# A gated cross-attention and a quantised feed-forward stage in one program block: general path first, two tiles in the last batch's attention

## The chip, the cores and the metric

The kernel runs on one core of a Trainium2 chip. The metric is device microseconds from the start to the end of one execution; lower is better. The engines are named PE (matmul), PEld (its weight load), DVE, ACT, POOL (GpSimd) and SP, which here only issues DMAs.

## What is computed

```python
def bitlinear(x, w, b):
    xq = act_quant(rmsnorm(x))          # 8 bit levels per row
    wq = weight_quant(w)                # -1, 0, 1 times a mean
    return einsum('bsd,fd->bsf', xq, wq) + b
# x: (32, 224, 512), ctx: (32, 750, 384), 16 heads of 32
q = layernorm(x) @ Wq.T;  k, v = ctx @ Wkv.T
attn = where(pad_mask[:, None, :, None], q @ k.T * scale, -1e9)
x = x + tanh(g_xattn) * softmax(attn) @ v
x = x + tanh(g_ffn) * bitlinear(gelu(bitlinear(layernorm(x), w1, b1)), w2, b2)
```

The mask is per query row, and a masked row gets the mean of v. In the inputs that are timed only rows from 168 on can be unmasked, which is the last quarter of a batch.

## The kernel before

**Attention stage.** A batch of 224 rows is four blocks of 56 (`NBLK`, `R`). In each batch only the last block (`RB`), together with one row of zeros that gives the mean of v, is attended; two batches share one tile of x (`xa`, 114 rows). `period(b, j, t, late)` on each engine does batch b's attention and, woven into it, batch b+1's projection to k and v. The projections and scores split each fp32 operand into a high and a low part (`y_h`, `y_l`, `wkv_h`, `wkv_l`, `k_h`, `k_l`), three matmuls each. `batches` calls `period` for all 32 batches; the last two are written out. The last has no projection to do. Heads come in four groups, and for each group the order is: scores on PE; the maxima on DVE (`negated_max`); exp on ACT (`softmax`); transposes of prob on PE (`turn_prob`); their copies to `prob_t` by ACT (`first_half`) and DVE (`second_half`); `weighted` sums on PE; `heads_out` on DVE. `sums` and `divided` end a batch. PE's scores of group g+1 wait for both copies of group g.

POOL and DVE also normalise the previous batch's rows for the feed-forward stage (`summed`, `centred`, `rounded`, `x1_moments`, `x1_peak`) and SP stores them in DRAM as x1 rows and quantised xq rows. In the second half POOL also rounds the weights (`weights`) into `w_q`, one piece a batch.

**General path.** A batch with unmasked rows in other blocks goes through `slow`, which is held in a loop over 32 batches behind two tests (class `Slow`). `most` is the largest of the flags `kind`; each engine loads it and jumps over the loop if it is at most 1, as it is here. `most` comes from the mask by a DVE reduction (`live_b`), a DMA that brings that onto one partition (`live`), and three small DVE operations. In the kernel before, these three stand behind `wkv_l` on DVE, and `Slow` stands at the end of the first block.

**Feed-forward stage.** It is a second `nc.Block`, behind a barrier, over 56 tiles of 128 rows. In step s, PE widens tile s (16 matmuls, L1556), transposes tile s-2's integers (L1566), transposes the next input (L1575), and narrows tile s-3 (16 matmuls, L1583). DVE copies the widened halves to `hid` (L1498), ACT applies GELU (L1455), takes the integers (L1462) and the squares (L1468). Widening needs `xq_t` of the tile, and `hid` needs `b1_row`, the bias in all partitions (1024 KB) times a factor. A tile's xq is 128 KB and its x1 256.5 KB.

Every engine runs its instructions in the order of the code, and all waits are on semaphores. SP is one queue too: its DMAs go out in the order in which it meets them. Its first are y (1125 KB), two halves of wkv (768 KB each), wq (1024 KB), two gates (0.5 KB each), b2 (224 KB), and then `live` (0.5 KB).

## Time and profile before

| | us |
|---|---|
| median of three runs | 1872.94 (1870.43 to 1877.92) |
| the profiled execution | 1872.22 |
| its span | 1870.4 |
| PE busy | 1807.6 |
| DVE / ACT / POOL busy | 1155.2 / 990.6 / 791.2 |

All times in the rows further down are counted from the start of the span. Three stretches matter: the first 20 us, in which inputs land and PE starts; 1348 to 1427 us, from the start of the last batch's attention to the feed-forward tile 4; and the long steady loops on both sides of it.

### The profile page before, as it was taken

Reading aid. Unit: us, or ns where it says so; the run is one execution under the profiler, and the core shown is the slowest. Engines: PE = TensorE matmul, PEld = TensorE weight load, DVE = VectorE, ACT = ScalarE, POOL = GpSimd, SP = SyncE. Lnnn points to the kernel's source line nnn. Section 1 sums busy time; section 2 is a strip of 40 time slices with the busy share of each in tenths; the row PEclk is TensorE's granted clock in tenths of the full one; section 3 lists DMA queues with packets and bytes.
Section 4 is the critical chain, followed back from the end, with each engine's and each line's share of the span. In section 5 each row is a group of like instructions: output and inputs, shape, how many; then the busy total and the mean of one; then the engine's idle time right before and its main releaser. Section 6 shows DMA issues by size and latency. Waiting matters only on the chain. (4 is left out here: it accounts for less than half of the span.)

```text
span 1870.4 us, 46291 instructions
## 1 busy us (share of the span) xinstructions
PE 1807.6 (97%) x16938; PEld 1396.5 (75%) x16995; DVE 1155.2 (62%) x2015; ACT 990.6 (53%) x1639; POOL 791.2 (42%) x1091
## 2 busy tenths in 40 slices
PE   6999999999999999999999999999958999999998
PEld 6888888888888888888888888888834555555554
DVE  3555655555555655555555555555448888888885
ACT  3444444444444443444444444444327888888886
POOL 1134454443344453665556565655444222222222
PEclk9999999999999999999999999999979999999999
DMA  4132222322332222322332222322242222222221
GB/s 157 35 96 85 73 78 73 92 73 80 117 89 78 73 78 75 94 73 78 110 93 83 73 78 73 92 73 78 66 132 66 80 85 81 76 82 84 81 75 45
DMA packets 83697, 154.24 MB, mean 82 GB/s; under 512 B 9726, under 2 KB 24062, under 8 KB 83510
## 3 DMA queue, kind: packets, MB, share of 16 engines
q1 hardware_dynamic: 83310, 153.24, 27.2%
q8 instruction: 33, 0.54, 0.1%
q10 hardware_dynamic: 328, 0.25, 0.1%
q14 instruction: 26, 0.21, 0.0%
HBM read 112.99 MB, written 40.81 MB: 82 GB/s over the span
## 5 line engine op out<-in xcount | busy, mean ns | idle before, releaser
L593 ACT ACTIVATE prob<-psum,nmax 114x750 f32<-114x750 f32 x256 | 225.5, 885 | 268.0 <-DVE nmax L766 268.0
L771 DVE TENSOR_TENSOR k_l<-psum,k_h 128x376 fp32r<-128x376 f32 (+1 forms) x256 | 139.8, 546 | 286.7 <-ACT k_h L584 286.7
L766 DVE TENSOR_REDUCE nmax<-psum 114x1 f32<-114x750 f32 x256 | 228.5, 934 | 80.2 <-PE psum L1025 79.4
L1036 PE MATMUL psum<-y_h,wkv_h 128*128 128x376 f32 (+1 forms) x768 | 276.7, 360 | 1.1 <-DVE q_l L759 1.1
L584 ACT ACTIVATE k_h<-psum 128x376 fp32r<-128x376 f32 (+1 forms) x256 | 123.9, 484 | 280.7 <-PE psum L1036 280.0
L1036 PE MATMUL psum<-y_l,wkv_h 128*128 128x376 f32 (+1 forms) x768 | 255.6, 333 | 0.0
L1036 PE MATMUL psum<-y_h,wkv_l 128*128 128x376 f32 (+1 forms) x768 | 255.4, 333 | 0.0
L1046 PE MATMUL psum<-wkv_h,y_h 128*125 128x512 f32 x576 | 237.8, 413 | 0.7 <-DVE wkv_l L823 0.7
L264 POOL TENSOR_TENSOR f_x<-f_c,f_x 112x512 f32<-112x512 f32 x64 | 76.3, 1193 | 361.0 <-DMA f_c<-vmean_rows 337.6
L1046 PE MATMUL psum<-wkv_l,y_h 128*125 128x512 f32 x576 | 228.8, 397 | 0.0
L1046 PE MATMUL psum<-wkv_h,y_l 128*125 128x512 f32 x576 | 228.0, 396 | 0.0
L1556 PE MATMUL psum<-w_q,xq_t 128*128 128x512 bf16 x894 | 207.3, 386 | 9.5 <-DVE xq_t L1527 9.3
L1056 PEld LDWEIGHTS psum<-ident,prob 114*125 114x125 f32 x1536 | 187.2, 190 | 12.0 <-ACT prob L593 3.3
L1583 PE MATMUL psum<-w_q,hq_t 128*128 128x512 bf16 x842 | 191.1, 379 | 5.1 <-ACT yo L1477 2.2
L1056 PE MATMUL psum<-ident,prob 114*125 114x114 f32 x1536 | 190.2, 274 | 4.8 <-ACT prob L593 4.8
L780 DVE COPY prob_t<-psum 125x342 f32<-125x342 f32 x256 | 128.4, 512 | 104.3 <-PE psum L1056 93.5
L1556 PEld LDWEIGHTS psum<-w_q,xq_t 128*128 128x128 bf16 x896 | 85.0, 99 | 126.4 <-issue 22.3
L1455 ACT ACTIVATE hid<-hid,gelu_in 128x1024 f32<-128x1024 f32 x112 | 128.0, 1144 | 83.8 <-DVE hid L1498 83.5
L459 POOL TENSOR_TENSOR y_l<-y,y_h 128x750 fp32r<-128x750 f32 x93 | 151.0, 1650 | 26.4 <-ACT y_h L579 26.4
L1423 POOL TENSOR_SCALAR cols<-cols 128x1 f32<-128x1 f32 x56 | 10.7, 191 | 346.8 <-ACT junk L1468 346.8
L1583 PEld LDWEIGHTS psum<-w_q,hq_t 128*128 128x128 bf16 x896 | 85.2, 98 | 95.4 <-ACT yo L1477 2.8
L1036 PEld LDWEIGHTS psum<-y_h,wkv_h 128*128 128x128 f32 x768 | 144.6, 188 | 14.6 <-DVE q_l L759 1.5
(120 smaller groups left out, 3372.7 us busy)
## 6 DMA issues: line engine op xcount, KB each, us to landing
y<-in_ctx_t SPq DMA_DIRECT2D x32, 1125.0 KB, 5.7
w_part<-in_w_t SPq DMA_DIRECT2D x32, 512.0 KB, 7.1
x_rows<-f_x SPq DMA_DIRECT2D x64, 224.4 KB, 2.7
x<-x_rows SPq DMA_DIRECT2D x56, 256.5 KB, 2.7
f_x<-in_x SPq DMA_DIRECT2D x64, 224.0 KB, 5.4
out_rows<-yo SPq DMA_DIRECT2D x56, 256.0 KB, 2.1
xq_rows<-f_q SPq DMA_DIRECT2D x64, 112.0 KB, 2.6
xq<-xq_rows SPq DMA_DIRECT2D x56, 128.0 KB, 2.2
```

The costliest lines, as they stand in the source:

```text
L459: pool.tensor_tensor(y_l[:, slot, c, :], y[:, c, :], y_h[:, slot, c, :].bitcast(F32), ALU.subtract).then_inc(a_yl, 1)
L584: act.activation(k_h[:, g, s0:s1], ps_proj[k_bank[par][g, hf]][:, 0:s1 - s0], ACT.Copy).then_inc(a_kh, 1)
L593: act.activation(prob[:, e, :], ps_score[e][0:RP], ACT.Exp, bias=nmax[:, i:i + 1], accum_out=den[:, i:i + 1]).then_inc(p.exp, 1)
L766: dve.tensor_reduce(nmax[:, i:i + 1], ps_score[e][0:RP], AX.X, ALU.max, negate=True).then_inc(p.max, 1)
L771: dve.tensor_tensor(k_l[:, g, s0:s1], ps_proj[k_bank[par][g, hf]][:, 0:s1 - s0], k_h[:, g, s0:s1].bitcast(F32), ALU.subtract).then_inc(a_k ...
L780: dve.tensor_copy(prob_t[:, g % 2, e, MH:MJ, :].rearrange("p j n -> p (j n)"), ps_pt[e][1]).then_inc(p.pd, 1)
L1036: mm = pe.matmul(out_, ws[:, c, w], ys[:, slot, c, s0:s1], start=(c == 0 and n == 0), stop=(c == CC - 1 and n == 2))
L1046: mm = pe.matmul(out_, ys[:, slot, c, mcols], ws[:, c, D:], start=(c == 0 and n == 0), stop=(c == CC - 1 and n == 2))
L1056: mm = pe.transpose(ps_pt[e][hf][:, RP * j:RP * j + RP], prob[:, e, MC * jj:MC * jj + MC], ident[0:RP, 0:RP])
L1455: act.activation(seg, seg, ACT.Gelu, scale=gelu_in[:, 0:1]).then_inc(t_g, 1)
L1556: mm = pe.matmul(ps_h[i][:, BANK * o:BANK * o + BANK], xq_t[:, j % 2, 128 * c:128 * c + 128], w1_q[:, c, at_:at_ + BANK], start=(c == 0), ...
L1583: mm = pe.matmul(ps_y, hq_t[:, (j - LAG) % 2, 128 * c:128 * c + 128], w2_q[:, c, :], start=(c == 0), stop=(c == FC - 1))
```

## The change

1. Both stages stand in one `nc.Block`. Class `Slow` is called ahead of `batches` on every engine, with its own set of semaphores (`Flow("s")`) and its own results in DRAM (`x1_slow`, `xq_slow`), which SP copies over the main ones later (`copies`, `copy_one`), if there are any.
2. DVE computes `live_rest`, `kind` and `most` ahead of its first statistics.
3. The last batch is a function `final()` on each engine. It holds the attention of batch 31 and the widening of tiles 0 and 1, one half of a tile for each group of heads, in PSUM banks that the projection has left free (`ps_h_early`, `ps_x_early`). The feed-forward buffers share memory with the projection's, so SP loads them once the projection is done.
4. The general steps then run from step 2. `squares` writes its unused output into `hq`. The normalisation of batch 31 moves to steps 3 to 7 and its stores to step 48. There is no vmean fill of attn_rows.

```diff
@@ DVE, at the beginning @@
 dve.tensor_reduce(live_b[:], ..., AX.X, ALU.max).then_inc(a_flag, 1)
+dve.wait_ge(a_live, 16)
+dve.tensor_reduce(live_rest[:], live[:, :, 0:NBLK - 1], AX.X, ALU.max).then_inc(a_flag, 1)
+dve.wait_ge(a_flag, 2)
+dve.scalar_tensor_tensor(out=kind[:], in0=live_rest[:], scalar=2.0, in1=live[:, :, NBLK - 1],
+                         op0=ALU.mult, op1=ALU.max).then_inc(a_flag, 1)
+dve.wait_ge(a_flag, 3)
+dve.tensor_reduce(most[:], kind[:], AX.X, ALU.max).then_inc(a_flag, 1)
@@ every engine (here PE) @@
-batches(pe, period, middle)
 slow_pe = Slow(pe, "pe")
-slow_pe.each(slow)
+slow_pe.each(B, slow_first, slow, slow_finish)
+batches(pe, period, middle, final)
+run_steps(pe, step, EARLY, NT + LAG)
@@ SP, from batch 30's results on @@
+copier = Slow(sp, "copy")
+copier.each(B - 2, copies_first, lambda b, n: copies(b, c_st), copies_finish)
+sp.wait_ge(main.k, 2 * NG * B + ONE)
+sp.wait_ge(main.v, MJ * B + ONE)
+sp.wait_ge(last.q, B // 2 + ONE)
+sp.wait_ge(a_yl, CC * B + ONE)
+step(-2, -2, 0)
+sp.dma_start(b1_row[:], one_row(b1).to_broadcast([128, F])).then_inc(b_bias, 16)
+step(-1, -1, 0)
+stored(B - 2)
+ffn_load(B - 2, B - 2, False)
+w2_piece(B - 1, B // 8 - 1, 1)
+step(0, 0, 0)
+ffn_store(B - 2, B - 2)
+results(B - 1)
 stored(B - 1)
-sp.dma_start(rows(attn_d, B - 1, 0, RB), vmean_d[B - 1:B, :].to_broadcast([RB * R, D])).then_inc(a_fill, 16)
...
+run_steps(sp, step, 1, NT + LAG + 2)
@@ POOL @@
+def final():
+    for part in (summed, centred, rounded):
+        for h in range(2):
+            part(B - 2, h)
+    step(1, 1, 0)
+    weights(B - 1)
@@ ACT @@
+def squares(s, j):
...
+    if exists(s - 2):
+        act.wait_ge(t_ht, 2 * (s - 2) + 2)
+    act.activation(hq[:, j % 2, 0:F // 2].bitcast(BF16), hid[:, j % 2, :], ACT.Square, ...)
+def final():
...
+    for e in range(2):
+        softmax(last, n0, NG - 1, e)
+    gelu(0, 0, 0)
+    gelu(0, 0, 1)
+    for e in range(2):
+        first_half(last, n1, NG - 1, e)
+    squares(0, 0)
+    gelu(1, 1, 0)
+    gelu(1, 1, 1)
+    integers(1, 1)
+    squares(1, 1)
@@ PE, final(), group 1 @@
+    scores(last, 1, 1)
...
+    pe.wait_ge(a_wuse, 3 * (B // 4) + ONE)
+    widened(0, 0, 0)
+    weighted(last, n0, 1, 0)
+    turn_prob(last, n0, 1, 0)
+    turn_prob(last, n0, 1, 1)
+    turn_out(last, b, 0)
+    inputs(1, 1, 0)
```

On DVE at the beginning, this is the order before (`live_b` is the reduced mask, `x_stats` the statistics of the first x tile):

```order
L736 TENSOR_REDUCE live_b<-w_q 32x4 [waits a_mrow]
L742 BN_STATS x_stats<-xa 114x6 [waits p0_x,a_head,a_zero]
L744 BN_AGGR x_mv<-x_stats 114x2 [waits own_dve]
L745 ISA
L814 CAST mcol<-mcol 114x128 [waits a_mask]
L817 TENSOR_TENSOR y_l<-y,y_h 128x750 [waits a_yh] x3
L750 TENSOR_TENSOR x_keep<-x_rstd,mcol 114x1 [waits p0_rstd,a_mcol]
L752 TENSOR_SCALAR xa<-xa,x_mv,x_keep 114x512 [waits own_dve]
L753 ISA
L823 TENSOR_TENSOR wkv_l<-w_q,wkv_h 128x3x512 [waits a_whi] x2
L825 TENSOR_REDUCE live_rest<-live 1x32 [waits a_live]
```

And this is it in the changed kernel, on the same engine at the same place:

```order
L977 TENSOR_REDUCE live_b<-w_q 32x4 [waits a_mrow]
L979 TENSOR_REDUCE live_rest<-live 1x32 [waits a_live]
L981 SCALAR_TENSOR_TENSOR kind<-live_rest,live 1x32 [waits a_flag]
L984 TENSOR_REDUCE most<-kind 1x1 [waits a_flag]
L990 BN_STATS x_stats<-xa 114x6 [waits p0_x,a_head,a_zero]
L992 BN_AGGR x_mv<-x_stats 114x2 [waits own_dve]
L993 ISA
L1062 CAST mcol<-mcol 114x128 [waits a_mask]
L1065 TENSOR_TENSOR y_l<-y,y_h 128x750 [waits a_yh] x3
L998 TENSOR_TENSOR x_keep<-x_rstd,mcol 114x1 [waits p0_rstd,a_mcol]
L1000 TENSOR_SCALAR xa<-xa,x_mv,x_keep 114x512 [waits own_dve]
```

The wait on `a_live` has moved from behind `wkv_l` to ahead of all that DVE does for PE's first work.

On DVE in the last batch, the order before is (`nmax` the maxima, `prob_t` the copies that scores wait for, `f_stats` batch 30's statistics):

```order
L766 TENSOR_REDUCE nmax<-psum 114x1 [waits p0_s] x2
L780 COPY prob_t<-psum 125x342 [waits p0_pt] x2
L766 TENSOR_REDUCE nmax<-psum 114x1 [waits p0_s] x2
L784 COPY o_t<-psum 128x57 [waits p0_o]
L267 BN_STATS f_stats<-f_x 112x6 [waits f_x1]
```

In the changed kernel DVE has there (`b_row` is b1_row, named as the profile names it):

```order
L1014 TENSOR_REDUCE nmax<-psum 114x1 [waits p0_s] x2
L1272 TENSOR_SCALAR b_row<-b_row,bias_out 128x2048 [waits b_bias]
L1028 COPY prob_t<-psum 125x342 [waits p0_pt] x2
L1235 COPY xq_t<-psum 128x512 [waits t_xt]
L1014 TENSOR_REDUCE nmax<-psum 114x1 [waits p0_s] x2
L1032 COPY o_t<-psum 128x57 [waits p0_o]
L343 BN_STATS f_stats<-f_x 112x6 [waits a_x1]
L345 BN_AGGR f_mv<-f_stats 112x2 [waits own_dve]
L346 ISA
L1213 SCALAR_TENSOR_TENSOR hid<-psum,x,b_row 128x1024 [waits t_h,b_x10,b_b1]
L1028 COPY prob_t<-psum 125x342 [waits p0_pt] x2
```

The wait for the bias load stands between the maxima and the copies of group 0, and a widened half between two groups.

On PE at group 1 of the last batch, the order before is (`k_l,q_h` and so on are scores, `prob_t,v` the weighted sums, `ident,prob` the transposes):

```order
L1025 MATMUL psum<-k_h,q_l 114x238 x2
L1065 MATMUL psum<-prob_t,v 32x57 [waits p0_pa,a_vd,p0_pd,a_va,p0_on]
L1065 MATMUL psum<-prob_t,v 32x57 x23
L1056 MATMUL psum<-ident,prob 125x114 [waits p0_exp]
L1056 MATMUL psum<-ident,prob 125x114 x5
L1056 MATMUL psum<-ident,prob 125x114 [waits p0_exp]
L1056 MATMUL psum<-ident,prob 125x114 x5
L1073 MATMUL psum<-ident,o_t 57x128 [waits p0_oe]
```

In the changed kernel PE has at the same place:

```order
L1372 MATMUL psum<-k_h,q_l 114x238 x2
L1618 MATMUL psum<-w_q,xq_t 128x512 [waits a_wuse,t_xe,a_vd,a_va]
L1618 MATMUL psum<-w_q,xq_t 128x512 x7
L1412 MATMUL psum<-prob_t,v 32x57 [waits p0_pd,p0_pa]
L1412 MATMUL psum<-prob_t,v 32x57 x23
L1403 MATMUL psum<-ident,prob 125x114 [waits p0_exp]
L1403 MATMUL psum<-ident,prob 125x114 x5
L1403 MATMUL psum<-ident,prob 125x114 [waits p0_exp]
L1403 MATMUL psum<-ident,prob 125x114 x5
L1420 MATMUL psum<-ident,o_t 57x128 [waits p0_oe]
L1629 MATMUL psum<-ident_b,xq 128x128 [waits t_xe,b_xq1]
L1629 MATMUL psum<-ident_b,xq 128x128 x3
```

Eight widening matmuls now stand between the scores and the weighted sums, and the transposes of the next input behind them.

## Rows read from the trace of the kernel before

**Rows 1.** The page, PE: busy us, share of the span, instructions, then the weight loads and others

```profile
PE 1807.6 (97%) x16938; PEld 1396.5 (75%) x16995; DVE 1155.2 (62%) x2015; ACT 990.6 (53%) x1639; POOL 791.2 (42%) x1091
```

**Rows 2.** Windows: length; PE, PEld, DVE, ACT, POOL busy; clock, DMA share, GB/s

```profile
1348.00:1366.00 18.00, 13.81 (x160) 10.80 (x158) 10.21 (x18) 6.38 (x14) 7.83 (x12) 0.63 0.30 88
...
1427.04:1788.40 361.36, 358.91 (x2269) 185.95 (x2312) 306.03 (x444) 295.61 (x268) 88.66 (x144) 1.00 0.27 82
```

**Rows 3.** Timeline of PE, last batch: start, us, operation, count, idle before

```profile
1354.53 0.97 PE L1025 MATMUL psum<-k_h,q_h 64*114 64x512 f32 x4 [0.70 <-DVE prob_t L780]
...
1362.32 0.97 PE L1025 MATMUL psum<-k_h,q_h 64*114 64x512 f32 x4 [0.48 <-DVE prob_t L780]
...
1369.02 0.60 PE L1025 MATMUL psum<-k_h,q_h 64*114 64x512 f32 x4 [0.59 <-DVE prob_t L780]
...
1370.24 0.81 PE L1065 MATMUL psum<-prob_t,v 125*32 125x57 f32 x48
1372.33 1.78 PE L1056 MATMUL psum<-ident,prob 114*125 114x114 f32 x12 [1.27 <-ACT prob L593]
...
1376.25 0.38 PE L1077 MATMUL psum<-den,ident 114*57 114x8 f32 x4
```

**Rows 4.** The chain of waits that ended last, at the seam: start, us, what

```profile
1387.06 4.84 DMA b_row<-in_b
...
1391.92 1.30 DVE b_row L1484
...
1398.80 1.28 ACT L1455
...
1400.09 2.20 ACT hid L1455 x2
...
1405.70 0.21 DVE cols L1507
...
1406.38 1.29 DVE hid L1498
...
1408.75 2.08 ACT hq L1462
...
1417.32 5.31 PE psum L1556 x16
```

**Rows 5.** Timeline of PE, tile 4 of the feed-forward stage

```profile
1427.04 3.62 PE L1556 MATMUL psum<-w_q,xq_t 128*128 128x512 bf16 x16
```

**Rows 6.** Timeline of PE, its first projection

```profile
14.81 0.76 PE L1046 MATMUL psum<-wkv_h,y_h 128*125 128x512 f32 x1 [0.72 <-DVE wkv_l L823]
```

**Rows 7.** The page's DMA issues: count, KB each, median us to landing

```profile
live<-live_b SPq DMA_DIRECT2D x1, 0.5 KB, 12.1
```

**Rows 8.** Timeline of DVE at the beginning

```profile
8.71 0.69 DVE L742 BATCH_NORM_STATS2 x_stats<-xa 114x6 f32<-114x512 f32 x1 [5.14 <-DMA xa<-in_x]
...
12.91 3.42 DVE L823 TENSOR_TENSOR wkv_l<-w_q,wkv_h 128x1536 fp32r<-128x1536 f32 x2
18.33 0.24 DVE L825 TENSOR_REDUCE live_rest<-live 1x32 int32<-1x96 int32 x1 [2.00 <-DMA live<-live_b]
...
19.08 0.17 DVE L830 TENSOR_REDUCE most<-kind 1x1 int32<-1x32 int32 x1
```

**Rows 9.** Lines 213 and 216, PE's sequencer: ns min/median/max, first and last start

```profile
L213 PEldq TENSOR_LOAD <-most x1: 697/697/697, 1376.3 to 1376.3; - x1
...
L216 PEldq COMPARE_BRANCH  x1: 3795/3795/3795, 1377.2 to 1377.2; - x1
```

**Rows 10.** Timeline of SP's DMA queue in the last batch

```profile
1351.02 0.33 SPq L345 DMA_DIRECT2D f_x<-in_x  x1
```

**Rows 11.** Timeline of DVE, last batch, and the peak of tile 0

```profile
1349.64 1.78 DVE L766 TENSOR_REDUCE nmax<-psum 114x1 f32<-114x750 f32 x2 [0.17 <-PE psum L1025]
1352.66 0.52 DVE L780 COPY prob_t<-psum 125x342 f32<-125x342 f32 x1 [1.23 <-PE psum L1056]
...
1402.31 2.29 DVE L1530 TENSOR_REDUCE cols<-hid 128x1 f32<-128x2048 f32 x1 [1.59 <-ACT hid L1455]
```

995 lines of the change are left out of this document (558 added, 437 removed).

## The prediction

> **What bounds the kernel now.** I read the page's engine shares first: PE is busy for 97% of the span [rows 1], so time is to be had only where PE stands still or runs at its lower clock. The windows say where that is [rows 2]. Over the 361 us of the feed-forward loop PE is busy for 358.9 us at a granted clock of 1.00, and the projections and attention before 1348 us look the same. In the last batch's attention (1348 to 1366 us) no projection of a next batch fills the gaps: PE is busy for 13.8 of 18 us at a mean granted clock of 0.63, a mixture of the 1.2 and the 2.4 GHz level. Then comes the seam. PE's last attention work starts at 1376.25 us [rows 3]. After it the chain of waits puts the first 4.84 us after the barrier on the b1_row load, then 1.30 us of DVE, a 1.28 us table load, GELU, and so on [rows 4]. Tile 4 starts at 1427.04 [rows 5], and from there PE is continuous. The two numbers to watch are therefore the start of PE's first real work (14.81 us [rows 6]) and the start of tile 4 (1427.04). Between them, and behind tile 4, the change leaves the work as it is.
>
> **At the beginning: a loss of 10.6 us.** The general path needs `most`, and `most` needs the little copy `live`. That copy is 0.5 KB, yet it took 12.1 us from issue to landing [rows 7], since SP issues it behind y, both halves of wkv, wq, the gates and b2. DVE could use it at 18.33 us and had `most` at 19.08 + 0.17 = 19.25 [rows 8]. Before, this stood behind everything that PE waits for at the beginning, and cost nothing. Now the three reductions stand ahead of DVE's first statistics. In the trace those start at 8.71 us, xa is ready 4.2 us later (wkv_l starts at 12.91), and PE's first projection follows at 14.81 [rows 6, 8]. Moved behind 19.25, all of it comes 19.3 - 8.7 = 10.6 us later, because DVE is a single queue and y_l, the normalised xa and wkv_l all stand in it. The next `y` load of SP waits for y_l and moves by the same amount.
>
> Each engine must also load `most` and take the jump over the general path. On PE these took 0.70 us and 3.80 us at the old place [rows 9]. They can start at 19.25 and so end at 23.8. PE has nothing to do before xa at 12.91 + 0.1 + 10.6 = 23.6, and its first real work, which waits for half of wkv_l, is due at 14.81 + 10.6 = 25.4. I count nothing, with 0.5 us as the upper bound. DVE jumps after wkv_l (12.91 + 3.42 + 10.6 = 26.9 us), when its next input still has to come from PE's first projections. The cover is the very delay just counted. If the copy landed early, PE's jump would be the next thing late, about 4.6 us after `most`.
>
> As to bounds of this term: the copy queues behind loads that are unchanged, so 18.3 is the likely landing. The only traffic behind it in time is the next `y` load, which before was issued once y_l was done (before 12.91) and now goes out after the copy. If that had held the copy up, it could land 2 us sooner. So 8.8 to 11.1 us, and I take 10.6. The Trainium skill, in "DMA: Bandwidth & Descriptors", section "Two DMAs through the same engine are not ordered", says that within one queue of one DMA engine the descriptors start in the order of issue. By this rule the later y load can't have held the copy up, and the lower end would be 10.6 instead of 8.8; no row here tells the two apart, and the range keeps 8.8.
>
> **At the seam: removed.** The drain and barrier of the first block, the vmean fill of the last batch, the exposed b1_row load and GELU's table load all leave the path. I don't add them up, since they partly overlap; I build the new path and compare the starts of tile 4.
>
> **At the seam: the new path.** SP issues the loads for tile 0 and b1_row after results(30). The load of `most` and the short jump cost it about 1.3 us, about as long as the landing of vmean that it waited for anyway. So the first tile load goes out near 1351.1, where f_x went before (1351.02 [rows 10]), and b1_row, the third load, near 1352.0. It took 4.84 us for 1024 KB [rows 4]; the 385 KB of tile 0 ahead of it are 1.8 us at that rate and have a head start of 0.9, so I add 0.9 and get 1357.7. **Here the change adds a wait**: DVE stops for b1_row (final() has it behind the first two maxima) and queued behind it are the copies of prob_t, for which PE's next scores wait. Before, the first of these copies ran at 1352.66 and took 0.52 us [rows 11]. Now 1357.7 + 1.30 for the product [rows 4] + 2 x 0.52 for the copies = 1360.0, and the scores of group 1 start at 1360.1 instead of 1354.53 [rows 3], 5.6 us late. PE is idle meanwhile, except for four small transposes.
>
> From there a group took 6.70 us at mostly the upper level (1362.32 to 1369.02 [rows 3]). Half a tile of widening adds eight matmuls to PE and one 1.29 us operation to DVE [rows 4]. PE's part lies beside DVE's maxima (1.78 us [rows 11]), DVE's part fills about half of its own waiting, so I take 7.2 us per group: scores at 1360.1, 1367.4 and 1374.4. The last stretch, from the scores of group 3 to the denominators, took 1376.25 - 1369.02 = 7.2 us [rows 3]. ACT now puts the table load (1.28) and tile 0's GELU (2.20) [rows 4] ahead of the prob_t copies, so 10.7 us, and the attention ends at 1385.1. I allow DVE 1.5 us for the division, then it takes the peak of tile 0 (2.29 [rows 11]) and the columns (1405.70 to 1406.38, 0.7 [rows 4]), and ACT starts tile 0's integers at 1389.6. From these integers to tile 3 on PE the trace shows 1417.32 - 1408.75 = 8.57 us [rows 4]; the order of the work in between is the same. Tile 3 starts at 1398.2 and tile 4 one period of 8.1 us later, at 1406.3. That is 20.7 us before 1427.04, with PE at the upper level throughout.
>
> It won't be. The 1348 to 1366 window had 0.63 [rows 2], and now PE first stands still for 5 us. A group's PE operations at the upper level are scores 1.2 and weighted sums 0.8, transposes 1.8 [rows 3] and widening 1.8 (half of a tile's 3.62 [rows 5]); DVE's maxima hide some 2 of these 5.6 us, so 3.5 us a group lie on the path, 14 us in four groups. The lower level doubles them. If it holds for about a quarter of that, 3.7 us are lost. Another 1 us goes where PE stands still before tile 3, since the tile there ran at the lower level before as well (5.31 us for 16 matmuls, against 3.62 for the 16 of tile 4 [rows 4, 5]). **Gain at the seam: 20.7 - 3.7 - 1.0 = 16.0 us**, with bounds of 4.4 (the lower level all the way, and b1_row landing 2.3 us later) and 22.1 (the upper level, landing 2.2 us sooner).
>
> The rest: squares now writes into hq instead of junk and takes over a wait for the transposes of tile s-2, which PE finishes some 4 us earlier. Batch 31's own normalisation moves two steps later and its store to step 48, both far ahead of step 52, which reads it. Nothing for either. The end of the loop is unchanged.
>
> **Sum.** 10.6 - 16.0 = -5.4 us. The profiled execution took 1872.22 us (span 1870.4, 1.8 around it), which gives 1866.8. It lies 0.7 below the median of 1872.94, so I forecast 1867.5.
>
> **Rivals.**
> (a) PE's clock stays at the lower level all through the weave. For it: the window at 0.63, and a first idle stretch that is longer than before. Against it: by 1366 us the trace was back at the upper level, and PE now has 32 more large matmuls in this stretch. All 14 us of PE work on the path double, and the gain shrinks to 20.7 - 14.0 - 1.0 = 5.7. Then 10.6 - 5.7 gives +4.9, so 1878, slower than before. With a later b1_row it is 1880. It decides from the point where the seam gives less than 10.6. The Trainium skill, in "TensorE: Matmul & The Clock Gate", section "Part 4: PE-mode transpose", says that transposes don't count as activity for the clock in the way that matmuls do; that speaks for this rival, and no row here separates it.
> (b) The upper level throughout, and b1_row on time: -20.7 + 10.6 = -10.1, so 1863; with the copy 1.8 us sooner, 1861. For it: the woven matmuls fill exactly the gaps that let the clock fall.
> (c) The copy `live` lands much sooner, at 14 us, because nothing follows it. The delay is then set by PE's jump, 4.6 us after `most`, and is about 7 us: 10.6 - 7 = 3.6 us less, so 1864. Against it: the eight loads ahead of it are unchanged.
>
> **How the numbers follow.** Forecast 0.58 (its own range is 1863.5 to 1873), (a) 0.15, (b) 0.17, (c) 0.10. Eight times in ten that is 1861 to 1877. A measurement of this kernel can tell about 0.5%, 9.4 us, from no change, so faster means below 1863.6. To that (b) gives 0.12, (c) 0.04 and the forecast 0.04: 0.20. Slower means above 1882.3, which only the far end of (a) reaches: 0.04. Within 0.5%: 0.76.
>
> **What would show it.** In the changed profile: PE's first projection near 25.4 us (a start before 20 refutes the loss); DVE idle on the live copy for some 14 us, then statistics at 19.3; DVE idle some 6 us on b1_row in the last batch, with the second scores 11.8 us after the first; no gap of over 8 us on PE at the seam; tile 4 some 1427.0 + 10.6 - 16 = 1421.6 us after the span's start. A granted clock near 1.0 through the last batch would mean (b), one near 0.5 (a). The forecast is wrong if the main loops change length, since I took them as equal.

## The result and the profile after

| | before | changed |
|---|---|---|
| median | 1870.43 us (11 runs, 1866.06 to 1877.92) | 1867.0 us (11 runs, 1865.39 to 1869.8) |
| span of the profiled execution | 1870.4 | 1865.9 |
| first projection on TensorE | 14.81 | 22.75 |
| first scores of the last batch | 1348.30 | 1359.74 |
| tile 4 on TensorE | 1427.04 | 1422.82 |

The ratio of the changed kernel to the kernel before is 0.9974, with a 95% interval of 0.9965 to 0.9984. That is 4.9 us in 1870, less than half of a per cent, and clearly not zero; the two medians differ by 3.4 us, since the kernel before scatters by over 11 us. In a second comparison it was 0.9979 (0.997 to 0.9987).

The page gives the same answer to [rows 1] as before, 97% for PE, and doesn't tell where anything went:

```profile
PE 1808.0 (97%) x16994; PEld 1395.2 (75%) x16995; DVE 1154.2 (62%) x2015; ACT 990.6 (53%) x1639; POOL 793.4 (43%) x1091
```

What does tell is one event that both programs have once in every batch: SP's store of attn_rows. The table gives the time of this store in the changed kernel, less the time of the same store in the kernel before. A step in it is a place where time was lost or won.

| store of batch | before, us | changed, later by | |
|---|---|---|---|
| 0 | 86.85 | 8.82 | the beginning |
| 15 | 716.36 | 9.21 | |
| 16 | 760.44 | 14.49 | + 5.3: the middle of the batches |
| 29 | 1305.85 | 14.80 | |
| 30 | 1349.03 | 11.43 | - 3.4: the exit of the second loop |
| end of the span | 1870.4 | - 4.5 | the seam: - 15.9 |

**The beginning.** Timeline of the changed kernel (start, duration, engine, line, operation, idle time before it and what ended it). The answers to [rows 6] and [rows 8] are here: DVE stands for 12.51 us on `live`, then come `most` and the statistics, and SP's second y load goes out behind y_l. The first projection is 7.9 us later than before, and the store of batch 0 8.8 us; the 0.9 us between the two is not followed further.

```profile
6.14 0.79 SPq L399 DMA_DIRECT2D live<-live_b  x1
...
15.86 0.24 DVE L979 TENSOR_REDUCE live_rest<-live 1x32 int32<-1x96 int32 x1 [12.51 <-DMA live<-live_b]
...
16.37 0.17 DVE L984 TENSOR_REDUCE most<-kind 1x1 int32<-1x32 int32 x1
16.48 0.69 DVE L990 BATCH_NORM_STATS2 x_stats<-xa 114x6 f32<-114x512 f32 x1
...
20.20 0.41 SPq L405 DMA_DIRECT2D y<-in_ctx_t  x1
...
21.45 0.99 PE L1356 MATMUL psum<-ident,xa 114*128 114x114 f32 x4 [21.45 <-DVE xa L1000]
...
22.75 0.76 PE L1393 MATMUL psum<-wkv_h,y_h 128*125 128x512 f32 x1 [0.30 <-DVE wkv_l L1071]
```

PE's jump over the general path is the sequencer's row of line 260, which answers [rows 9] (count, ns min/median/max, start):

```profile
L260 PEldq COMPARE_BRANCH  x1: 3845/3845/3845, 17.2 to 17.2; - x1
```

**The middle.** Behind batch 15 the program leaves the first loop and computes the scales of the weights. DVE then stands for 6.45 us with nothing to wait for; in the kernel before, a stall of 2.29 us is in the same place, one instruction earlier. First the changed kernel, then the kernel before:

```profile
727.07 0.20 DVE L1202 TENSOR_SCALAR y_out<-w_mean,gates 128x1 f32<-128x1 f32 x1
733.72 0.69 DVE L990 BATCH_NORM_STATS2 x_stats<-xa 114x6 f32<-114x512 f32 x1 [6.45 <-issue]
```

```profile
720.27 0.21 DVE L961 TENSOR_SCALAR y_out<-w_mean,gates 128x1 f32<-128x1 f32 x1 [2.29 <-issue]
```

**The seam.** PE in the last batch of the changed kernel, as in [rows 3] and [rows 5]. Between the first scores and those of group 1 it is idle for 5.59 us at a stretch, which ends with DVE's copy of prob_t. The widening (L1618) is the woven work; its first half tile runs at 3.59 us for 8 matmuls, the others at 1.90. The denominators are L1424.

```profile
1359.74 0.60 PE L1372 MATMUL psum<-k_h,q_h 64*114 64x512 f32 x4
...
1370.65 0.97 PE L1372 MATMUL psum<-k_h,q_h 64*114 64x512 f32 x4 [5.59 <-DVE prob_t L1028]
...
1372.80 3.59 PE L1618 MATMUL psum<-w_q,xq_t 128*128 128x512 bf16 x8
...
1380.53 0.60 PE L1372 MATMUL psum<-k_h,q_h 64*114 64x512 f32 x4 [1.57 <-DVE prob_t L1028]
...
1386.85 0.59 PE L1372 MATMUL psum<-k_h,q_h 64*114 64x512 f32 x4 [0.85 <-DVE prob_t L1028]
...
1396.70 0.38 PE L1424 MATMUL psum<-den,ident 114*57 114x8 f32 x4
...
1412.42 6.00 PE L1618 MATMUL psum<-w_q,xq_t 128*128 128x512 bf16 x16 [4.13 <-DVE xq_t L1235]
...
1422.82 2.54 PE L1618 MATMUL psum<-w_q,xq_t 128*128 128x512 bf16 x11
```

DVE explains the first stall: it waits for b1_row, whose load SP had issued at 1363.25. The later stop of 2.26 us stands between two column operations with nothing to wait for, and delays tile 0's integers, which end PE's idle time before their transposes:

```profile
1368.37 1.28 DVE L1272 TENSOR_SCALAR b_row<-b_row,bias_out 128x2048 f32<-128x2048 f32 x1 [5.54 <-DMA b_row<-in_b]
...
1403.32 0.21 DVE L1227 TENSOR_SCALAR cols<-cols,y_out 128x1 f32<-128x1 f32 x1 [2.26 <-issue]
```

The windows that answer [rows 2] (length; PE, PEld, DVE, ACT, POOL busy; granted clock, DMA share, GB/s) show a mixture of both clock levels in the first 18 us and the upper level in the next 18, where the woven matmuls run:

```profile
1358.00:1376.00 18.00, 10.28 (x61) 6.36 (x59) 7.72 (x12) 4.97 (x11) 3.20 (x3) 0.72 0.64 211
1376.00:1394.00 18.00, 15.58 (x240) 10.82 (x239) 13.82 (x24) 8.52 (x15) 10.43 (x20) 0.99 0.07 21
```

### The profile page after: what moved, and what is told of

It is laid out like the page before. It is cut to its first block, busy times and chain, and to the rows that moved or that the text cites. A ratio compares the mean times of both kernels' runs of the same rounds, so it can differ in the third digit from the quotient of the medians.

```text
span 1865.9 us, 46309 instructions
## 1 busy us (share of the span) xinstructions
PE 1808.0 (97%) x16994; PEld 1395.2 (75%) x16995; DVE 1154.2 (62%) x2015; ACT 990.6 (53%) x1639; POOL 793.4 (43%) x1091
## 4 chain that ended last, share of the span: by engine, by line
PE 89%; issue 3%; DVE 3%; ACT 2%; DMA 1%; POOL 1%; SPq 0%; POOLq 0%; DVEq 0%; ACTq 0%
PE psum L1383 23%; PE psum L1393 22%; PE psum L1403 9%; PE psum L1372 8%; PE psum L1618 8%; PE psum L1660 8%; PE psum L1412 5%; PE psum L1363 3%; PE psum L1646 2%; ACT hq L895 2%; DVE hid L1213 1%; PE psum L1420 1%; PE psum L1424 1%; DMA live<-live_b 1%; PE psum L1629 0%
## 5 line engine op out<-in xcount | busy, mean ns | idle before, releaser
L1618 PE MATMUL psum<-w_q,xq_t 128*128 128x512 bf16 x896 | 207.3, 385 | 4.1 <-DVE xq_t L1235 4.1
L1660 PE MATMUL psum<-w_q,hq_t 128*128 128x512 bf16 x896 | 202.6, 379 | 2.2 <-ACT yo L912 2.2
L1618 PEld LDWEIGHTS psum<-w_q,xq_t 128*128 128x128 bf16 x896 | 84.6, 99 | 120.5 <-issue 21.5
```

The source lines that it names most:

```text
L1618: mm = pe.matmul(out_[:, BANK * o:BANK * o + BANK], xq_t[:, j % 2, 128 * c:128 * c + 128], w1_q[:, c, at_:at_ + BANK], start=(c == 0), sto ...
L1660: mm = pe.matmul(ps_y, hq_t[:, (j - LAG) % 2, 128 * c:128 * c + 128], w2_q[:, c, :], start=(c == 0), stop=(c == FC - 1))
```

## The experiments

All times of stores below are again later than in the profile of before. The ratio to the kernel before is that of timed runs; a single profiled execution of one and the same kernel can lie over 4 us off its median. The last but one row shows where that scatter is: `e_before_y_late` is the kernel before with one wait more in its first 16 us, its stores up to batch 30 are within 0.03 us of those of before, and yet it is 3.6 us longer. All of that lies behind batch 30. So for one kernel the marks up to batch 30 can be read to some 0.2 us, and the end of the span only to some 4 us.

| kernel | ratio to before (95%) | batch 0 | 15 | 16 | 29 | 30 | end of span |
|---|---|---|---|---|---|---|---|
| changed | 0.9974 (0.9965 to 0.9984) | 8.8 | 9.2 | 14.5 | 14.8 | 11.4 | -4.5 |
| changed, again (`e_changed`) | 0.9979 (0.997 to 0.9987) | 8.7 | 9.1 | 14.3 | 14.6 | 11.2 | -4.4 |
| `e_live_act` | 0.994 (0.9928 to 0.9953) | 3.6 | 4.0 | 9.4 | 9.7 | 6.4 | -9.9 |
| `e_dve_order` | one execution | 8.0 | 8.4 | 15.3 | 15.6 | 12.2 | -5.2 |
| `e_mid_wait` | 0.995 (0.9937 to 0.9963) | 7.6 | 8.0 | 9.3 | 9.6 | 6.3 | -9.8 |
| `e_b1_late` | 0.9978 (0.9967 to 0.9988) | 7.7 | 8.1 | 11.7 | 12.0 | 8.6 | -6.6 |
| `e_b1_early` | 0.996 (0.9944 to 0.9977) | 7.8 | 8.2 | 11.8 | 12.1 | 8.8 | -13.0 |
| `e_no_weave` | 1.0017 (1.0007 to 1.0027) | 8.0 | 8.4 | 15.2 | 15.5 | 12.1 | +4.4 |
| `e_pad` | one execution | 8.1 | 46.3 | 49.9 | 50.2 | 46.8 | +34.0 |
| `e_pad_half` | one execution | 9.3 | 10.0 | 13.2 | 30.5 | 27.1 | +9.9 |
| `e_two` | 0.993 (0.9918 to 0.9942) | 4.0 | 4.5 | 5.9 | 6.2 | 2.8 | -10.1 |
| `e_before_y_late` | one execution | 0.0 | 0.0 | 0.0 | 0.0 | 0.0 | +3.6 |
| `e_best` | 0.9893 (0.9878 to 0.9908) | 2.7 | 3.1 | 4.8 | 5.1 | 1.7 | -21.9 |

### The changed kernel once more

> The changed kernel once more, beside the others on one chip: its place among them, and how far its stall at the middle differs between two profiles. That stall was 6.4 us in two profiles of kernels with the same code up to there and about 4 to 5 in others. Expected: 0.997 to 0.998 of the kernel before, and marks within 2 us of the first profile's.

Measured: 0.9979, DVE's stall at the middle 6.42 us, and every mark within 0.2 us of the first profile. So steps of 1 us and more in the table are differences between kernels. (A mark can still differ by about a microsecond at the beginning between kernels whose code is the same there: 7.6 to 8.8.)

### The beginning: the copy `live` from another queue

```diff
@@ SP @@
-sp.wait_ge(a_flag, 1)
-sp.dma_start(live[:], live_b[:]).then_inc(a_live, 16)
@@ ACT, behind the loads of mcol8 @@
+act.wait_ge(a_flag, 1)
+act.dma_start(live[:], live_b[:]).then_inc(a_live, 16)
```

> Undoes the cause of the start loss. The copy of live_b to one partition is issued from ACT's queue, at about 3.6 us, instead of SP's, where it stood at 6.14 behind the two halves of wkv, wq, the gates and b2 and was used at 15.86. Theory (the 7.94 us by which the first projection came later are the time of that copy plus the jump of 3.8 us behind it): live is used by 7 us, most is there by 7.5, PE's jump ends by 12 beside the loads, DVE's x_stats and y_l no longer stand behind the copy, PE's first projection is at 14.8 to 15.8 and the kernel is 7 to 8 us faster than the changed kernel, about 1859. Rival 1 (the copy waits for the DMA engines, not for its queue): live is still used after 13 us and less than 3 us are gained. Rival 2 (the other engines' jumps, DVE's behind wkv_l above all, then take the place): the first projection is at 15 but the first results come 3 to 4 us later than in the kernel before, and 4 us are gained.

```profile
4.64 0.63 ACTq L731 DMA_DIRECT2D live<-live_b  x1
...
11.10 0.24 DVE L978 TENSOR_REDUCE live_rest<-live 1x32 int32<-1x96 int32 x1 [6.49 <-DMA live<-live_b]
...
11.61 0.17 DVE L983 TENSOR_REDUCE most<-kind 1x1 int32<-1x32 int32 x1
...
17.31 0.99 PE L1355 MATMUL psum<-ident,xa 114*128 114x114 f32 x4 [17.31 <-issue]
...
17.98 0.77 PE L1392 MATMUL psum<-wkv_h,y_h 128*125 128x512 f32 x1
```

Measured: 0.994, 11 us below the kernel before and 6.4 us better than the changed kernel by the ratios; the marks give 5.2 at batch 0. The theory's chain is right (the projection moved from 22.75 to 17.98 with `most`, which moved from 16.54 to 11.78), but not its size: even on ACT's queue, behind five loads of x and the mask only, the 0.5 KB took 6.5 us to land, not some 3. SP's large loads are in flight then (from 4 to 11 us the DMA engines are busy throughout, at 290 to 410 GB/s); that these are the reason is likely, not shown. And PE's jump, 4.46 us here, is now the last thing PE waits for (17.31, "issue").

### The beginning: DVE's order or PE's jump

```diff
@@ DVE @@
-dve.wait_ge(a_live, 16)
-dve.tensor_reduce(live_rest[:], ...)
...
-dve.tensor_reduce(most[:], kind[:], AX.X, ALU.max).then_inc(a_flag, 1)
 dve.wait_ge(a_zero, 3)
...
     dve.tensor_tensor(wkv_l[:, :, w], ..., ALU.subtract).then_inc(a_wlo, 1)
+dve.wait_ge(a_live, 16)
+dve.tensor_reduce(live_rest[:], ...)
...
+dve.tensor_reduce(most[:], kind[:], AX.X, ALU.max).then_inc(a_flag, 1)
```

> The changed kernel with DVE's reading of live, kind and most put back behind both halves of wkv_l, where the kernel before has it; PE and the others still branch on most ahead of their first work. Theory D (of the prediction: DVE's x_stats, y_l and wkv_l behind the landing of live set the first projection): wkv_l is ready by 17 us and PE starts its first projection at once, 4 to 6 us earlier than in the changed kernel, at 17 to 19 us. Theory J (most, PE's load of it, 0.5 us, and its jump, 3.8 us, set it): most is ready at 17 to 18.5, a little later than now (16.5), and PE's first projection is at 22.5 to 24, no earlier than the 22.75 of the changed kernel.

```profile
13.02 3.42 DVE L1064 TENSOR_TENSOR wkv_l<-w_q,wkv_h 128x1536 fp32r<-128x1536 f32 x2
...
16.86 0.17 DVE L1071 TENSOR_REDUCE most<-kind 1x1 int32<-1x32 int32 x1
...
21.74 0.99 PE L1356 MATMUL psum<-ident,xa 114*128 114x114 f32 x4 [21.74 <-issue]
...
22.41 0.77 PE L1393 MATMUL psum<-wkv_h,y_h 128*125 128x512 f32 x1
```

```profile
L260 PEldq COMPARE_BRANCH  x1: 3641/3641/3641, 17.7 to 17.7; - x1
```

Measured: theory J. wkv_l was ready over 5 us before PE's first projection, and yet that started at 22.41, 0.3 us sooner than in the changed kernel. `most` at 17.03, the load of it, and 3.64 us of jump set it. That is 5.38 us behind `most`; in the changed kernel, where `most` is there at 16.54, the jump alone would so allow 21.9, an estimate, and DVE's order made it 22.75. The two limits lie within a microsecond of each other, so that removing one alone brings less than that. The Trainium skill gives a compare-and-branch 108 ns ("Advanced Engine Details and Errata", section "Control Flow Timing"); The other engines' rows at this jump have 45 to 56 ns, about half of it; PE's jump over the general path is far from it: 3.64 to 4.46 us in these three kernels. It says elsewhere ("Runtime: NRT & Kernel Launch", section "Instruction fetch mechanics") that a branch out of the fetched instructions has to wait for them; that would be this case.

### The beginning: what held the copy up

In the kernel before, and nothing else of it changed:

```diff
@@ SP, kernel before @@
+sp.wait_ge(a_live, 16)
 ahead(-1, 1, -1)
```

> The kernel before with one wait more: SP issues the second y load only when live has landed. In the kernel before that load went out at 12.44 us and live was used at 18.33; in the changed kernel it goes out at 20.2 and live is used at 15.86. Theory (the y load's packets share the DMA engines with the copy of live and hold it up, though the copy was issued first): live is in use by 16.7 us (DVE is at wkv_l until 16.5). Rival (DVE's order, or the end of the gates' and b2's loads, sets it): still at 18 to 18.7.

```profile
15.77 0.41 SPq L329 DMA_DIRECT2D y<-in_ctx_t  x1
...
16.20 0.23 DVE L826 TENSOR_REDUCE live_rest<-live 1x32 int32<-1x96 int32 x1
```

Measured: live was in use at 16.20, as soon as DVE was free, and had landed by 15.77, when SP went on. With the y load issued at 12.44, 3.3 us sooner, it was 18.33 [rows 8]. So a load issued some 6 us *behind* the copy held it up by 2.5 us or more. The prediction took the rule that it cites, by which descriptors start in the order of issue, to exclude this. Nothing here speaks against the rule itself, but it says only when transfers start, not when one that runs beside a megabyte of others has landed; for that the measurement decides.

### The middle: the instruction fetch and the loads

```diff
@@ SP, ahead of the first y load behind batch 15 @@
     whole = B // 8 if i < 3 else B // 8 - 2
+    if i == 2:
+        sp.wait_ge(last.mv, B // 4 + 2 + ONE)
```

> At the middle of the batches SP holds the y load (and what stands behind it) until DVE has passed its first moments behind the middle. Between y_out at 727.07 and x_stats at 733.72 DVE stood for 6.45 us with nothing to wait for in the profile, where the kernel before stood 2.29 us at the same place; SP's loads are issued at 726.9 to 731.7. Theory C (DVE waits for its own instructions, and their fetch shares the DMA engines with those loads): the stall is 2 to 3 us and the kernel 3.5 to 4.5 us faster, about 1863. Theory P (the length of the stall goes with where the code lies, whatever the engines carry): it stays at 6 to 7 us; the time is the same, or up to 1 us longer for the later y.

```profile
730.12 0.70 DVE L992 BATCH_NORM_STATS2 x_stats<-xa 114x6 f32<-114x512 f32 x1 [4.11 <-issue]
```

Measured: 0.995, and the step between batches 15 and 16 fell from 5.3 to 1.4 us, 3.9 us less, as expected. Theory C, though not in all: the stall is 4.11 us, not 2 to 3, so this much of it is there with nearly idle DMA engines, and 2.3 us came from the loads. From 726 to 730 us the only packets on them are three of the queues named "instruction", one of 16.4 KB and two of 8 KB; which of them DVE waited for no record says. The rest of the gain is behind it: with the longer stall PE ran out of work and stood another 2.9 us for `prob`. `e_two` and `e_best`, which hold the loads too, have stalls of 4.20 and 4.38 us and steps of 1.5 and 1.7. The step without the hold is less regular: in `e_b1_late` and `e_b1_early` it is only 3.6 us behind stalls of 6.35 and 6.38, in `e_dve_order` and `e_no_weave` 6.8 to 6.9 behind 7.20 and 7.06, though nothing was edited there. What sets the part beyond DVE's stall is open, so some 2 us of such a step are no effect of an edit.

### Where the code lies

Two kernels got instructions that never run, in the general path of DVE (memsets) and of PE (transposes): 128 on either engine, and 64.

```diff
@@ DVE, slow_first() @@
+for _ in range(128):
+    dve.memset(xs, 0.0)
@@ PE, slow() @@
+for _ in range(64):
+    pe.transpose(ps_xt[:, 0:RP], ident[0:RP, :], ident[0:RP, 0:RP])
```

> The changed kernel with 128 instructions more in DVE's general path and 128 in PE's (64 transposes with their weight loads), none of which runs: every instruction behind them lies that much further on in the program, and nothing else changes. Theory (the stalls at the loop's exits depend on where the code lies): PE, which ran through the exit into batch 30 without a stop in the changed kernel and stood 1.6 to 1.9 us after three of the four first scores in the kernel before, changes there, so that the result of batch 30 is not 3.4 us nearer to that of before than batch 29's; at the middle DVE's stall begins behind another instruction than y_out. Rival (the stalls come from what goes on in the program at these points): DVE's stall begins behind y_out, PE has none at batch 30, and all the marks are within 1.5 us of the changed kernel's.

> The changed kernel with 64 instructions more, not 128, in the general paths of PE (32 transposes with their weight loads) and of DVE; none runs. With 128 more, PE read instructions in every turn of the first loop (76 packets of its instruction queue up to 800 us, of 16.4 KB each, against 16), stood still for 2.4 and 1.2 us at the turn's start while the y load had the DMA engines, and the kernel took 40 us longer; DVE's stall, whose queue's packets are of 8 KB, was behind the same instruction. Theory (what counts is where the loop's bounds lie in pieces of that size): with 64 more, DVE's stall at the middle moves off its place behind y_out; PE's loop either fits as now (8 to 10 us of shift at batch 15) or reads in every turn as with 128 (some 46 us). Rival (any shift of PE's code makes it read in each turn by growth): a shift between, 20 to 30 us, and DVE's stall still behind y_out.

I had not expected the size. With 128 more the kernel took 1906.14 us in one execution, and nearly all of the loss is in the first loop: 3.9 to 6.6 us in each turn from the second on, 37 in all. PE's rows at the start of such a turn, and the windows around it:

```profile
140.40 0.60 PE L1374 MATMUL psum<-k_h,q_h 64*114 64x512 f32 x4 [2.37 <-issue]
...
143.29 0.79 PE L1395 MATMUL psum<-wkv_l,y_h 128*125 128x512 f32 x1 [1.20 <-issue]
...
146.44 0.63 PE L1395 MATMUL psum<-wkv_h,y_l 128*125 128x512 f32 x1
```

```profile
142.00:145.00 3.00, 1.80 (x5) 1.41 (x5) 2.10 (x4) 0.98 (x2) 0.00 (x0) 0.57 1.00 375
```

PE stands for 2.4 us without a releaser while the DMA engines are nearly idle (SP's y load goes out only at 139.76, near its end), then for 1.2 us while they are full, and then runs its matmuls at 0.63 instead of 0.40 us for a time, at the lower clock (0.50 from 143 to 146 us). The instruction queue q8 in the same 800 us, first with 128 more, then in the changed kernel (packets, MB, share):

```profile
q8 instruction: 76, 1.25, 0.7%
```

```profile
q8 instruction: 16, 0.26, 0.1%
```

76 packets of 16.4 KB against 16. With 64 more, the first loop was as before (10.0 at batch 15) and the second one read in every turn: the marks climb from 13.2 to 30.5, in steps of 2.2 to 3.9 us, and q8 has 52 packets between 800 and 1300 us where the changed kernel has none. DVE's stall at the middle moved too, from behind y_out to another place, 2.4 us ahead of a copy of prob_t (q14, which had packets of 8 KB, is the other instruction queue in these windows):

```profile
728.38 0.69 DVE L990 BATCH_NORM_STATS2 x_stats<-xa 114x6 f32<-114x512 f32 x1 [0.32 <-DVE y_out L1202]
```

With 128 more, that stall was still behind y_out (6.37 us), and PE's passage into batch 30 was unchanged as well. So of what I had expected of the first of these kernels neither came; what came instead, the reading in every turn, led to the second kernel, and that one bore out its theory for the loops and for the place of the stall. That 128 instructions move DVE's place by exactly nothing fits packets of 8 KB, half of the 16.4 KB that PE reads. An estimate with the page's numbers fits: the Trainium skill ("Runtime: NRT & Kernel Launch", section "Instruction fetch mechanics") gives PE a store of 2048 instructions, filled in blocks of 256, which are 16 KB; that is the size of q8's packets here. A turn of the loop has 884 matmuls and 880 weight loads in the trace (1764, and the waits and branches besides), which is between 6.9 and 8 such blocks, so it fits in the store or just does not, by where its first instruction lies. The same section calls the cost of crossing a block mostly hidden. Here it was, until the loop no longer fitted; then it was 37 us.

The step of -3.4 us behind batch 29 this does not explain. In the kernel before, PE stands there for some 1.6 us after its third score and then runs at the lower clock; in the changed kernel and in all ten kernels derived from it the step is -3.3 to -3.4, with 0, 64 and 128 instructions more. Both profiles of the kernel before's code have the stop (1.58 and 1.60 us) and a packet of q8 just ahead of it, and the changed kernel has no such packet between 1295 and 1320 us; a read of instructions at the loop's exit is the likeliest cause, but no run tests it. Open is also the cause of the 0.4 us that creep in over the first sixteen batches.

### The seam: without the weave

The calls for tiles 0 and 1 are out of final() on every engine, and the general steps run from step 0:

```diff
-EARLY = 2
+EARLY = 0
@@ PE, final(), at its end @@
+pe.wait_ge(last.on, B + ONE)
+inputs(0, 0, 0)
@@ DVE, final(), at its end @@
+dve.wait_ge(b_bias, 16)
+dve.tensor_scalar(b1_row[:], b1_row[:], bias_out[:], 1.0, ALU.mult, ALU.mult).then_inc(b_b1, 1)
+dve.wait_ge(b_b1, 1)
+inputs(0, 0)
```

> Undoes the second part alone: the general path stays at the beginning, but the first two feed-forward tiles stand behind the last batch's attention again, as in the kernel before. Theory (the seam gives 15.7 us, which is the start's 7.9, the middle's 5.3 and 0.4 of creep less 3.4 at the loop's end, and then the 4.9 that are left): without the weave the kernel is 14 to 17 us slower than the changed one, at 1881 to 1884, and 9 to 12 us slower than the kernel before. Rival (a good part of the seam's gain is the removed copying and flag work between the two stages, not the overlap of TensorE's work with the waits of the last batch): it is under 8 us slower than the changed kernel.

```profile
1360.41 0.60 PE L1355 MATMUL psum<-k_h,q_h 64*114 64x512 f32 x4
...
1393.55 0.56 PE L1407 MATMUL psum<-den,ident 114*57 114x8 f32 x4
1396.03 0.61 PE L1612 MATMUL psum<-ident_b,xq 128*128 128x128 bf16 x4 [1.93 <-DVE attn L1033]
```

The same place in the kernel before:

```profile
1392.29 0.60 PE L1575 MATMUL psum<-ident_b,xq 128*128 128x128 bf16 x4 [15.66 <-DMA xq<-xq_rows]
```

And the window over the second half of the last batch without the weave:

```profile
1378.00:1396.00 18.00, 13.29 (x189) 11.02 (x187) 9.06 (x17) 6.79 (x13) 13.83 (x20) 0.50 0.13 39
```

Measured: 1.0017, about 8 us slower than the changed kernel and 3 us slower than the kernel before. Between the two expectations, and nearer to the rival's. The weave is worth 8 us, and the other 8 of the seam come from what the general path's new place removes: PE's gap at the seam is 1.93 us instead of 15.66, since b1_row, tile 0's rows and GELU's table are there already.

But this kernel's last batch is 5.2 us longer than that of the kernel before (33.1 us from the first scores to the denominators, against 27.95 [rows 3]). PE's clock stays at its lower level through its second half (0.50), where it came back in the profile of before (0.60 us for the scores of the last group, against 0.97 [rows 3]). That return is not a property of the kernel before. `e_before_y_late` has the same code there, with its first scores at 1348.32 against 1348.30, and its last group still ran at the lower level:

```profile
1370.01 0.97 PE L1026 MATMUL psum<-k_h,q_h 64*114 64x512 f32 x4 [0.48 <-DVE prob_t L781]
...
1378.73 0.55 PE L1078 MATMUL psum<-den,ident 114*57 114x8 f32 x4
```

Its last batch took 30.4 us, 2.5 more than in the first profile, and that by the clock alone. So 2.5 of the 5.2 us is a difference that two executions of one code show too. Of the rest 1.1 us is a longer wait for prob_t ahead of group 2 (1.63 us of idle time against 0.48), where DVE has batch 30's moments in between. The timed runs say the same: eight of the nine without the weave took 1874.8 to 1878.1 us at a mean clock of 0.985 to 0.990, and one took 1870.93 at 0.992. So the 8 us of the weave are probably in good part clock. In all eleven profiles with the woven matmuls the scores of the last group run at 0.60 us, and the twelve timed runs of `e_changed` lie within 1.9 us, while the seventeen of the kernel before beside them spread over 7 us, their mean clocks from 0.984 to 0.990. Why the clock comes back in one execution and not in another is not shown.

### The seam: b1_row

The first try moved only DVE's wait:

```diff
@@ DVE, final() @@
     negated_max(last, n0, 0, 1)
-    dve.wait_ge(b_bias, 16)
-    dve.tensor_scalar(b1_row[:], ...).then_inc(b_b1, 1)
...
     x1_moments(b - 1, 0)
+    dve.wait_ge(b_bias, 16)
+    dve.tensor_scalar(b1_row[:], ...).then_inc(b_b1, 1)
     dve.wait_ge(b_b1, 1)
```

> In the last batch DVE's wait for b1_row and its multiply stand behind inputs(0) and the maxima of head group 1, just ahead of the first use, instead of behind the first maxima. Theory (the 5.6 us for which PE stood idle ahead of the scores of group 1 are this wait, held in DVE's order ahead of second_half): the scores of group 1 follow the first scores by 5 to 6 us instead of 10.9, of which b1_row's landing at about 1368 takes nothing back, since the first widening is used only then; attention's end and every tile behind it come 3.5 to 5 us earlier, 1862 to 1863.5. Rival (the clock's or the widening's part decides: TensorE is then at its lower clock for longer, or the feed-forward tile in front of the weighting waits for b1_row anyway): the scores of group 1 are early, but those of group 2 are no more than 2 us earlier, and the kernel gains under 1.5 us.

```profile
1356.94 0.60 PE L1372 MATMUL psum<-k_h,q_h 64*114 64x512 f32 x4
...
1363.88 0.97 PE L1372 MATMUL psum<-k_h,q_h 64*114 64x512 f32 x4 [0.27 <-DVE prob_t L1028]
...
1376.07 0.97 PE L1372 MATMUL psum<-k_h,q_h 64*114 64x512 f32 x4 [5.12 <-DVE prob_t L1028]
```

Measured: 0.9978, no gain. The scores of group 1 came 6.9 us after the first, and the idle time of PE went to group 2, 5.12 us, where DVE now does the moments, the product (2.17 us) and the widening ahead of second_half(1). The stall was not removed but moved on by one group, and my expectation of 3.5 to 5 us fell.

The second try moves the load. b1_row lies in the memory of wq_s, which is last read in batch 29:

```diff
@@ SP, in batch 30 @@
     stored(b - 1)
+    if b == B - 2:
+        sp.wait_ge(last.q, B // 2 + ONE)
+        sp.dma_start(b1_row[:], one_row(b1).to_broadcast([128, F])).then_inc(b_bias, 16)
     ffn_load(b - 1, b - 1, False)
@@ SP, behind step(-2, -2, 0) @@
-sp.dma_start(b1_row[:], ...).then_inc(b_bias, 16)
```

> b1_row lies in the memory of wq_s alone, whose last reader is the query of the last pair, in batch 29: SP issues its load in batch 30, some 40 us earlier, instead of behind the copier's flag at the seam. DVE's order is that of the changed kernel. In the run that only moved DVE's wait, TensorE's idle time went from the scores of group 1 (5.6 to 0.3 us) to those of group 2 (1.6 to 5.1 us), for b1_row's use and the moments then stood ahead of second_half(1). Theory (the landing of b1_row is late, wherever DVE waits for it): the scores of group 1 follow the first by 7 us instead of 10.9, and of these 3.9 us at least 2.5 are left at attention's end, less what DVE's moments wait for POOL's f_x (it was summed 13.8 us behind the first scores): 2 to 3.5 us faster than the changed kernel, 1863.5 to 1865. Rival (POOL's f_x decides, whose loads stand behind the copier's flag just as b1_row did): group 1 is early, group 2 stays at 19 to 20.8 us behind the first scores, and under 1 us is gained.

```profile
1357.07 0.60 PE L1374 MATMUL psum<-k_h,q_h 64*114 64x512 f32 x4
...
1364.01 0.97 PE L1374 MATMUL psum<-k_h,q_h 64*114 64x512 f32 x4 [0.27 <-DVE prob_t L1030]
...
1372.71 0.60 PE L1374 MATMUL psum<-k_h,q_h 64*114 64x512 f32 x4 [1.68 <-DVE prob_t L1030]
...
1388.90 0.38 PE L1426 MATMUL psum<-den,ident 114*57 114x8 f32 x4
```

Measured: 0.996, 2.6 us better than the changed kernel by the ratios, though the intervals overlap. In the profile group 1 follows at 6.9 us and group 2 at 15.6 (20.8 in the changed kernel), and the denominators come 31.8 us after the first scores instead of 37.0. That profiled execution was the fastest of the six, so 5 us is its upper end.

### Both places, and all four edits

`e_two` has the edits of `e_live_act` and `e_mid_wait`. `e_best` has those and that of `e_b1_early`, and DVE's moments of batch 30's first half behind second_half(1):

```diff
@@ DVE, final() @@
     heads_out(last, b, 0)
-    x1_moments(b - 1, 0)
...
     inputs(1, 1)
+    x1_moments(b - 1, 0)
     x1_moments(b - 1, 1)
```

> Live from ACT's queue and SP's loads at the middle held, without the two edits at the seam. By the marks of the runs the first gives 4 to 5 us at the start and the second about 4 at the middle. Theory (places are independent): 8 to 9 us faster than the changed kernel, 0.993 to 0.9925 of the kernel before, and the other 6 to 8 us of the kernel with all four edits (0.9893) are the seam's. Rival (the seam's edits gave under 4 us, the timed gain of b1_row's earlier load alone being 0.14%): 0.991 or less.

> Four edits of one place each together: live from ACT's queue; SP's loads at the middle held until DVE is past it; b1_row loaded in batch 30; DVE's moments of batch 30's first half put behind second_half(1). The first two gave 0.34% and 0.24% over the changed kernel by their ratios to the kernel before (0.9940 and 0.9950 against 0.9974). If gains of separate places add up, they give 4 us each, and the seam's two edits 3 to 4 more: 11 to 12 us faster than the changed kernel, about 1856, 0.991 of the kernel before. Rival (they do not add: the seam's clock or POOL's f_x takes the last part): 8 us, 1859.

```profile
PE psum L1649 <- ACT hq L889: 5.8, 1, 5.8
...
PE psum L1375 <- DVE prob_t L1031: 1.6, 3, 0.6
```

Measured: `e_two` 0.993, 8 us faster than the changed kernel as expected; its two parts alone had 6.4 and 4.5 us by their ratios, 5.2 and 3.9 by the marks, so they add up by the marks (8.6 us at batch 30) and fall 2 to 3 us short by the ratios, about the width of the intervals. `e_best` has 0.9893 (0.9878 to 0.9908), a median of 1850.95 us. By the ratios that is 20 us faster than the kernel before and 15 to 16 faster than the changed one. It beats both, and the gain of the seam's two edits together, by the two ratios, is 6.9 us. In the wait list of its last batch PE's idle time for prob_t is down from 8.0 us to 1.6; the longest left is that for tile 0's integers, 5.8.

## Why the prediction was right, and where it was not

The forecast was 1867.5 us, 5.4 below the kernel before; measured were a median of 1867.0 and, by the ratio, 4.9 below. The seam was right in its sum. That the total was right to within half a microsecond was luck: the beginning was forecast 2.7 us too long, the main loops, taken as equal, were 2.6 us longer, with another 0.9 us between the first projection and batch 0's store, and these cancelled each other.

1. **The beginning, 10.6 us forecast, 7.9 measured** (first projection at 22.75, forecast 25.4), outside the bound of 8.8. The mechanism was the one named: DVE in one queue behind `live`, all of it later by the same amount. The term that was mis-sized is the landing: 18.3 forecast, 15.86 measured. The step that failed is "the copy queues behind loads that are unchanged, so 18.3 is the likely landing". The prediction did name the next y load as the one thing that moves, gave it 2 us, and took the other end; `e_before_y_late` shows that it was worth 2.5 us or more.
2. **The jump, counted at nothing.** Right in the sum. The warning beside it was right too: "If the copy landed early, PE's jump would be the next thing late, about 4.6 us after `most`". It ended at 21.1, 4.5 after 16.54, and with DVE's order out of the way (`e_dve_order`) the first projection came only 0.3 us sooner.
3. **The seam, 16.0 forecast, 15.7 measured** from the first scores to tile 4. Scores of group 1 were forecast 11.8 us after the first and came after 10.9; the stall for b1_row was forecast at some 6 us and was 5.6; the denominators were due 36.8 us after the first scores and came at 37.0. Between them the spacing was 9.9, 6.3 and 9.9 us where 7.2, 7.2 and 10.7 stood, since the lower clock lay in the first group alone. The 4.7 us taken off for the clock were right only as a sum: tile 0's integers came 2.8 us later than the path at the upper clock had them (2.26 of it is DVE's stop between two column operations, which was not in the sum), and tile 3, at the lower clock, took 10.4 us to tile 4 instead of 8.1. The price of the lower level, "doubles them", was too high for this work: the rows have 0.97 against 0.60 us for the same scores and 3.59 against 1.90 for half a tile of widening, 1.6 and 1.9 times. And the 15.7 is the gain against one execution of the kernel before; against `e_before_y_late` the same stretch is 16.6.
4. **What the gain is made of** the prediction left aside ("they partly overlap; I build the new path"). That was the safer way: `e_no_weave` splits it into 8 us of weave and 8 of work removed. In the 8 of the weave is the clock's return in the last batch, which came in every profile with it and, without it, in one execution of before and not in the other. I had expected 14 to 17 us of weave.
5. **"Main loops taken as equal"** was wrong by +5.3 at the middle, -3.4 at the second loop's exit and +0.7 of creep, +2.6 in all. The prediction said that it would be wrong if this didn't hold. Most of the +5.3 goes with DVE's stop of 6.45 us (2.29 before), and SP's loads at that moment are shown to set 2.3 us of its length. That the stop is a read of instructions fits its place, which moved with 64 never executed instructions, and the packets in it, but is an inference. The -3.4 is not explained.
6. **The rivals.** (a) The lower clock all through the weave did not happen: 0.72 in the first 18 us and 0.99 in the next. The Trainium skill's statement on transposes ("TensorE: Matmul & The Clock Gate", section "Part 4: PE-mode transpose"), which the prediction names beside it, is not refuted by that, for the widening's matmuls were what the last batch of `e_no_weave` (0.50) lacked; no run separates the transposes. (b) needed the upper clock throughout. (c) was half true: the copy landed 2.5 us sooner, not 4.

## What to carry to other kernels

Put one regular event of both programs side by side, here a store in each batch: it showed in one column what the shares of busy time and the total hid, and that an edit at the ends of a program had moved time in its middle. Take a second profile of the kernel before too: here the nearest thing to one, `e_before_y_late`, differed by 0.03 us for 1349 us and by 3.6 us behind that. When a wait that blocks an in-order queue is moved, ask what stands behind it at the new place, and better ask whether the load can start sooner. And a flag that every engine branches on belongs to the critical path by its landing *and* the jump: moving the small copy off the queue of the large loads was worth 0.34%, more than the change itself.
